# Moving four queues of a three-stage hybrid block onto tables of places, and B's rows into another buffer

## The chip, the cores and the metric

One core of a Trainium2 chip runs the whole program in one launch. The metric is the device time of one execution in microseconds, the median over timed runs. PE is TensorE, PEld its weight loads, DVE VectorE, ACT ScalarE, POOL GpSimd, SP SyncE.

## The reference

Sixteen sequences of 512 tokens of 256 numbers pass through attention, a routed feed-forward layer, a state-space layer, and the feed-forward layer again, each on the layer norm of x and added to x. All inputs are float32.

```
x = x + attention(layernorm(x))     # 16 heads of 16, causal softmax, RMS norm in front
x = x + ffn(layernorm(x))           # base + shared + 2 of 6 routed low-rank experts
x = x + ssm(layernorm(x))           # below
x = x + ffn(layernorm(x))
# ssm: xc = silu(conv4(x)); dt = softplus(xc Wd); B = xc Wb; C = xc Wc     (16 states)
#   h[n,t] = exp(a[n] dt[t]) h[n,t-1] + dt[t] xc[t] B[n,t];   y[t] = sum_n h[n,t] C[n,t]
#   out = (y * sigmoid(x Wg)) Wo
```

## The kernel before

**Frames and places.** The kernel is a software pipeline over the 16 sequences. Its clock is a count of places: 20 places are a group of four heads (10 score units of 2 places), 80 places (`FRAME`) one sequence. Each engine has its queue, written out in the order of places; a table per engine (`PE_AT`, `ACT_AT`, `DVE_AT`, `POOL_AT`, `SP_AT`) says at which place of a sequence a step is issued, and `due(now, at)` which sequence that concerns. Only the order comes from places; when something runs follows from the queues and the semaphores. While one sequence is in attention, the one before is in its state-space layer, and the heads' scores, the maxima and the exponentials (`max_unit`, `score_unit`, `exp_unit`) run between everything else.

**Attention.** Q and K are cast into three bfloat16 parts (`cast_part`, L826), which SP stores in DRAM (`store_parts`, L712) and loads as a stack (`stack`, L726). PE makes scores for the maxima (L372) and for the exponentials (L395); DVE reduces the first (L1026, L1028, L1023), and `finish_maxima` turns the maxima into rows `hlt` (L1044) that SP puts under the stack (`stack_maxima`, L733, four small transfers). ACT takes the exponentials (`pt`, L795), PE multiplies with V (L420).

**The state-space layer.** ACT copies B's 16 rows from a bank into `hwt` (`bc_high`, L878), SP stores them in DRAM (`store_b`, L737) and loads each row, spread over 128 partitions, into one of three buffers `b_all` (`load_b`, L747). ACT makes softplus (L903), DVE from it dt and u (`delta_u`, L1129 and L1131). For each of 16 states n: ACT makes the decays (`dec`, L910, two halves, buffers n % 2), POOL the inputs (`inp` = u times B, L1331 and L1337), DVE the scan (L1158), PE spreads C's row (L557), DVE multiplies (L1167), and POOL adds the product to y by an accumulating transfer (`add_state`, L1344). POOL's queue is in order: inputs 0 and 1 of a sequence stand before the last addition (n = 15) of the sequence before. Then `gate_y` (L1173) multiplies y with the gate and waits for that addition, PE applies the output weights (`ssm_out`, L321 and L323), and DVE adds to X (`add_and_sum`, L1081).

`hwt` is also the buffer for the weighted low-rank tokens of the feed-forward layer (`copy_weighted`, L862), so that copy waits for B's store.

The scans, decays, inputs, loads of B and the group's pieces are not in the tables: every engine's loop runs over groups q and units p, and small maps (`STEP_AT`, `PRODUCT_AT`, `DECAY_AT`, `FINISH`, `HEADS_PE`) say at which unit they stand. In SP's loop the store and first loads of B stand in the side work of unit 7, and the maxima behind it:

```
for now in (2 * (UN * q + p), 2 * (UN * q + p) + 1):
    ...
    if (a := due(now, SP_AT["store_b"])) >= 0:
        store_b(a)
        for n in range(3):
            load_b(NS * a + n)
if p == 7 and 0 <= q + 1 < NQ:
    stack_maxima(q + 1)
```

Of the kernel before, what the change touches and what calls it, by code (L numbers as in the profile page):

```python
# [7 lines left out]
ALU = mybir.AluOpType  # L8
# [48 lines left out]
def hybrid_block(nc, x, norm_w, wqk_t, bqk_c, wv_t, bv, wo_t, bo, conv_w, conv_b, wd_t, bd, wbc_t,  # L57
# [24 lines left out]
    LK = 32  # L82
# [6 lines left out]
    STEP_AT = {0: 0, 2: 1, 5: 2, 7: 3}  # L89
    PRODUCT_AT = {1: 0, 3: 1, 6: 2, 8: 3}  # L90
    DECAY_AT = {1: -1, 4: 0, 5: 1, 8: 2}
# [4 lines left out]
    FRAME = 2 * UN * NG  # L96
    PE_AT = {"res": (-32, -31), "xn": (-75, -71), "qk00": (-52, -50, -48), "qk01": (-50, -47, -44), "v": (-26, -32),
# [7 lines left out]
    ACT_AT = {"res": (-30, -28), "square_f": 98, "square_s": 127, "square_l": 252, "norm_q": -94, "norm_f": 103,  # L105
              "exp0": 115, "norm_s": 131, "softplus": 153, "decays": 160, "norm_l": 257, "exp1": 266,
# [4 lines left out]
    DVE_AT = {"add_x1": (94, 96), "in0": 113, "out0": 116, "add_up0": (123, 124), "silu": 144, "delta": 155,  # L111
              "gated": 246, "add_x3": (251, 251), "in1": 265, "out1": 268, "add_up1": (277, 280), "stats_q": -102}
    POOL_AT = {"rsqrt_f": 99, "rsqrt_s": 124, "rsqrt_q": -104, "inputs": 151, "rsqrt_l": 254, "low": (111, 266)}
    SP_AT = {"parts": (-43, -4), "load_x": -119, "store_b": 155, "store": 281}
    FINISH = 14
    HEADS_PE, HEADS_DVE = 4, 4

    ctx = ExitStack()
    with ctx:
# [88 lines left out]
        b_rows = hwt[0:NS, :]  # L208
# [94 lines left out]
        def _(pe):  # L303
# [246 lines left out]
            def spread_c(k):  # L550

                s, n = divmod(k, NS)
                if has(s):
                    pe.wait_ge(hc_done.sem, hc_done.at(s, n))
                    if n == 0:
                        pe.wait_ge(side["bc"].free, side["bc"].at("bc", s, 2))
                    mm(spread_bank[:, :], onehot[:, NS + n:NS + n + 1].to_broadcast([3 * NC, P]), bcs[:, s % 2, :],  # L557
                       start=True, stop=True).then_inc(c_ready.sem, 1)

            def spread_b(k):  # L560

                s, n = divmod(k, NS)
# [8 lines left out]
            def sum_y(k):  # L571

                s, n = divmod(k, NS)
                if has(s) and s >= LATE:
# [4 lines left out]
                    for c, m in enumerate(late_banks(s)):  # L579
                        last = mm(m[:, :], ident[:, :], hc[:, k % HC, c, :], start=(n == 0), stop=(n == NS - 1),  # L580
                                  skip_group_check=True)
# [72 lines left out]
            for q in range(FIRST, END):  # L654
                k = NG * q - LK
                if q == -2:
                    pe.wait_ge(dve_const, 1)
                for p in range(UN):
                    if 0 <= UN * q + p + LM < UN * NQ:
                        max_unit(UN * q + p + LM)  # L660
                    side_work(2 * (UN * q + p))
                    if 0 <= q < NQ:
                        score_unit(q, p)
                    if p in PRODUCT_AT:
                        spread_b(k + PRODUCT_AT[p] + 1)
                        spread_c(k + PRODUCT_AT[p])
                        sum_y(k + PRODUCT_AT[p] - 1)
                    if 0 <= q - 1 < NQ:
                        if p == 0:
                            values_b(q - 1)  # L670
                        elif p == 1:
                            values_c(q - 1)
                        if p == HEADS_PE:
                            turn_heads(q - 1)
                    if p == 7 and 0 <= q < NQ:
                        values_a(q)
                    side_work(2 * (UN * q + p) + 1)
# [3 lines left out]
        def _(sp):  # L681
# [57 lines left out]
            def load_b(k):  # L739

                s, n = divmod(k, NS)
                if has(s):
                    old_s, old_n = divmod(k - 3, NS)
                    sp.wait_ge(inp_ready.sem, inp_ready.at(old_s, old_n + 1))
                    if n < 3:
                        sp.wait_ge(b_stored.sem, b_stored.at(s))
                    sp.dma_start(b_all[:, k % 3, :], b_kept[s, n][None, :].to_broadcast([P, T])  # L747
                                 ).then_inc(b_loaded[k % 3].sem, 16)
# [11 lines left out]
            for q in range(FIRST, END):  # L760
                k = NG * q - LK
                for p in range(UN):
                    if p < 3 and 0 <= q + 2 < NQ:
                        stack(q + 2, p)
                    if p in STEP_AT and (k + STEP_AT[p]) % NS < NS - 3:
                        load_b(k + STEP_AT[p] + 3)
                    for now in (2 * (UN * q + p), 2 * (UN * q + p) + 1):
                        for j in range(2):
                            if (a := due(now, SP_AT["parts"][j])) >= 0:
                                store_parts(a, j)  # L770
                        if (a := due(now, SP_AT["store"])) >= 0:
                            store(a)
                        if (a := due(now, SP_AT["load_x"])) > 0:
                            load_x(a)
                        if (a := due(now, SP_AT["store_b"])) >= 0:
                            store_b(a)
                            for n in range(3):
                                load_b(NS * a + n)
                    if p == 7 and 0 <= q + 1 < NQ:
                        stack_maxima(q + 1)  # L780
# [4 lines left out]
        def _(act):  # L785
# [126 lines left out]

            def decays_ahead(k):
                s, n = divmod(k, NS)
                if has(s) and n + 2 < NS:
                    decays(s, n + 2)


            def side_work(now):
# [74 lines left out]
            for q in range(FIRST, END):  # L994
                k = NG * q - LK
                if q == -1:
# [5 lines left out]
                for p in range(UN):  # L1002
                    side_work(2 * (UN * q + p))
                    if 0 <= q < NQ:
                        exp_unit(q, p)
                    if p == 2 and 0 <= q - 1 < NQ:
                        copy_heads(q - 1)
                    if p in DECAY_AT:
                        decays_ahead(k + DECAY_AT[p])
                    side_work(2 * (UN * q + p) + 1)  # L1010
# [3 lines left out]
        def _(dve):  # L1014
# [125 lines left out]
            def scan(k):  # L1140
                s, n = divmod(k, NS)
                if k == NS * (NB - 1):
                    half_of_inputs(0)
                if has(s):
                    old_s, old_n = divmod(k - HC, NS)
# [122 lines left out]
            for q in range(FIRST, END):  # L1268
                if q == -4:
                    constants()  # L1270
# [164 lines left out]
```

## Time and profile before

| | |
|---|---|
| timed runs, median (lowest to highest) | 2170.35 us (2165.85 to 2177.23), 3 runs |
| profiled execution, first to last instruction | 2159.4 us, granted clock 0.956 |
| busy | PE 1842.8 us (85%), DVE 1684.1 (78%), ACT 1407.4 (65%), POOL 1040.1 (48%) |
| transfers | 275.53 MB, 128 GB/s; SP's queue 30.5%, POOL's 27.6% of 16 engines |

The profiled execution's own time is its span of 2159.4 us with the start and end of the program around it, which the profile doesn't show. The rows are of that one execution; times in them count from its first instruction. A number in brackets behind an instruction is how long its engine idled before it, and the name behind it is what ended that.

### The profile page before, as it was taken

The numbers are of one execution on the slowest core, as the hardware profiler recorded it, in microseconds if no ns is written. First come the engines' busy times: TensorE is split into PE (matmuls) and PEld (weight loads), VectorE is DVE, ScalarE is ACT, GpSimd is POOL, SyncE is SP. The second block draws the span as 40 slices with busy tenths as digits, with TensorE's granted clock in tenths as the row PEclk, the third lists the DMA queues.
The fourth block names the chain that finished last, engine by engine and source line by source line (L and its number), as shares of the span: only waits on it lengthen the run. The fifth ranks groups of instructions, "written<-read, shape, count | busy, mean of one in ns | idle before, by whom it ended". The sixth has DMA issues, their size and how long they took to land.

```text
span 2159.4 us, 33647 instructions
## 1 busy us (share of the span) xinstructions
PE 1842.8 (85%) x11409; PEld 1132.2 (52%) x11440; DVE 1684.1 (78%) x2586; ACT 1407.4 (65%) x2724; POOL 1040.1 (48%) x930
## 2 busy tenths in 40 slices
PE   5779888998989798988989898898989898877775
PEld 3446454645556464645556464655656464635333
DVE  5343678889788888879787888879887888987783
ACT  2445767686676767677675867677675767574531
POOL 0000364556555464646555464646555464666430
PEclk8999999999999999999999999999999999999998
DMA  4312377666767576667767686666767676652110
GB/s 115 83 52 59 93 152 153 145 142 150 159 140 159 124 170 140 151 128 154 158 148 157 129 171 130 146 142 149 156 141 157 133 157 135 139 112 61 45 59 10
DMA packets 185916, 275.53 MB, mean 128 GB/s; under 512 B 33537, under 2 KB 125586, under 8 KB 185746
## 3 DMA queue, kind: packets, MB, share of 16 engines
q1 hardware_dynamic: 155506, 163.27, 30.5%
q0 software_dynamic: 30240, 110.11, 27.6%
q8 instruction: 92, 1.51, 0.3%
q14 instruction: 78, 0.64, 0.1%
HBM read 128.58 MB, written 34.08 MB: 75 GB/s over the span
## 4 chain that ended last, share of the span: by engine, by line
PE 44%; ACT 19%; DMA 16%; SPq 7%; issue 6%; DVE 5%; POOL 2%; ACTq 0%; POOLq 0%; DVEq 0%
PE bank L314 7%; DMA sk<-qk_parts 7%; PE bank L518 5%; PE bank L323 5%; SPq L726 5%; ACT dec L910 3%; PE bank L372 3%; ACT pt L795 3%; PE bank L395 3%; PE bank L420 3%; PE bank L501 3%; DMA qk_parts<-parts 3%; DMA out<-X 3%; PE bank L482 3%; PE bank L308 2%
## 5 line engine op out<-in xcount | busy, mean ns | idle before, releaser
L1158 DVE TENSOR_TENSOR_SCAN hc<-dec,inp 128x1024 f32<-128x1024 f32 x256 | 613.1, 2395 | 33.0 <-ACT dec L910 28.6
L1331 POOL TENSOR_TENSOR inp<-u,b_all 128x512 f32<-128x512 f32 x256 | 341.1, 1332 | 421.9 <-DVE hc L1158 177.5
L795 ACT ACTIVATE pt<-bank 128x512 f32<-128x512 f32 x640 | 373.8, 597 | 220.4 <-PE bank L397 217.6
L372 PE MATMUL bank<-sk,sq 96*128 96x512 bf16 (+3 forms) x1024 | 279.6, 312 | 95.4 <-DMA sk<-qk_parts 64.4
L1337 POOL TENSOR_TENSOR inp<-u,b_all 128x512 f32<-128x512 f32 x240 | 350.0, 1458 | 18.8
L910 ACT ACTIVATE dec<-dt,a_neg 128x511 f32<-128x511 f32 x512 | 338.0, 717 | 31.4 <-DVE hc L1158 31.4
L1167 DVE TENSOR_TENSOR hc<-hc,bank 128x1024 f32<-128x1024 f32 x242 | 293.6, 1213 | 50.6 <-PE bank L557 49.9
L395 PE MATMUL bank<-sq,sk 98*128 98x512 bf16 (+3 forms) x1024 | 275.4, 307 | 34.1 <-ACT pt L795 28.1
L1344 POOL DMA_DIRECT2D y<-hc x210 | 185.6, 884 | 244.8 <-DMA y<-hc 122.9
L1026 DVE TENSOR_REDUCE mall<-bank 128x1 f32<-128x512 f32 x256 | 172.6, 674 | 100.3 <-PE bank L374 100.0
L372 PEld LDWEIGHTS bank<-sk,sq 96*128 96x128 bf16 x1024 | 102.3, 100 | 213.9 <-DMA sk<-qk_parts 73.0
L1028 DVE TENSOR_REDUCE mall<-bank 128x4 f32<-128x512 f32 x256 | 175.1, 684 | 44.8 <-PE bank L374 44.6
L374 PE MATMUL bank<-mask_qk,ident_bf 128*128 128x128 bf16 x1024 | 199.0, 226 | 0.0
L397 PE MATMUL bank<-mask_kq,ident_bf 128*128 128x128 bf16 x1024 | 196.7, 224 | 0.0
L420 PE MATMUL bank<-pt,v_sb 128*32 128x512 f32 (+3 forms) x2048 | 180.5, 448 | 0.0
L314 PE MATMUL bank<-xt_q,wqk 128*128 128x512 f32 x256 | 127.7, 623 | 42.4 <-ACT parts L826 22.9
L826 ACT ACTIVATE parts<-bank,bqk 128x512 bf16<-128x512 f32 x192 | 128.5, 689 | 53.2 <-PE bank L314 50.0
L395 PEld LDWEIGHTS bank<-sq,sk 98*128 98x128 bf16 x1024 | 102.6, 100 | 113.3 <-ACT pt L795 39.8
L1309 POOL TENSOR_TENSOR rs<-va,half 128x4 f32<-128x4 f32 x64 | 66.3, 1036 | 160.9 <-DVE ng L1068 156.9
L1081 DVE SCALAR_TENSOR_TENSOR X<-bank,X 128x256 f32<-128x256 f32 x192 | 73.2, 418 | 87.1 <-PE bank L502 45.3
L397 PEld LDWEIGHTS bank<-mask_kq,ident_bf 128*128 128x128 bf16 x1024 | 103.1, 101 | 49.2 <-issue 35.5
L1023 DVE TENSOR_REDUCE mall<-bank 128x2 f32<-128x512 f32 x128 | 87.9, 687 | 48.5 <-PE bank L374 48.3
(168 smaller groups left out, 3534.2 us busy)
## 6 DMA issues: line engine op xcount, KB each, us to landing
y<-hc POOLq DMA_DIRECT2D x210, 512.0 KB, 5.5
b_all<-b_kept SPq DMA_DIRECT2D x256, 256.0 KB, 4.0
qk_parts<-parts SPq DMA_DIRECT2D x96, 256.0 KB, 2.5
sq<-qk_parts SPq DMA_DIRECT2D x384, 64.0 KB, 3.6
sk<-qk_parts SPq DMA_DIRECT2D x384, 64.0 KB, 3.8
X<-in_x SPq DMA_DIRECT2D x16, 512.0 KB, 5.9
out<-X SPq DMA_DIRECT2D x16, 512.0 KB, 5.9
sq<-hlt SPq DMA_DIRECT2D x256, 2.0 KB
```

Source lines behind the costliest of these rows:

```text
L314: last = mm(dst[:, :], w[:, c, g * P:(g + 1) * P], src[:, c, :], start=(c == 0), stop=(c == C - 1))
L372: mm(dst[:, o:o + n], sq[0:KS, slot, h, qb * P:(qb + 1) * P], sk[0:KS, slot, h, 0:n], start=True, stop=False)
L374: return mm(dst[:, o + n - P:o + n], ident_bf[:, :], mask_qk[:, :], start=False, stop=True)
L395: mm(dst[:, o:o + n], sk[:, slot, h, kb * P:(kb + 1) * P], sq[:, slot, h, kb * P:T], start=True, stop=False)
L397: return mm(dst[:, o:o + P], ident_bf[:, :], mask_kq[:, :], start=False, stop=True)
L420: last = mm(pv_bank[VW * i:VW * (i + 1), kb * P:T], values_of(a, kb, first + i), pt[:, n % PT, at:at + T - kb * P], start=start, stop=stop ...
L795: A(pt[:, n % PT, :], score_bank[unit % 2][:, :], ACT.Exp).then_inc(exp_done.sem, 1)
L910: last = A(dec[:, n % 2, c, 1:T], dt[:, c, 1:T], ACT.Exp, scale=a_neg[:, c, n:n + 1])
L1158: V.tensor_tensor_scan(h, d, v, 0.0, ALU.mult, ALU.add).then_inc(scan_done.sem, 1)
L1167: V.tensor_tensor(hc[:, k % HC, :, :] if n or s >= LATE else y[:, s % 2, :, :], hc[:, k % HC, :, :], spread_bank[:, None, :].to_broadcast( ...
L1331: first = G.tensor_tensor(inp[:, n % 2, 0, :], u[:, 0, :], b_all[:, k % 3, :], ALU.mult)
L1337: G.tensor_tensor(inp[:, n % 2, 1, :], u[:, 1, :], b_all[:, k % 3, :], ALU.mult).then_inc(inp_ready.sem, 1)
```

## The change

The maps and the loops over q and p go; each engine runs over places `now`, and scans, products, decays, inputs, additions, loads of B, stacks, maxima, values and heads have rows in the tables, with `steps()` and `group()` beside `due()`. B's rows are copied into the first 16 partitions of `tok_f`, the normalised tokens' buffer, and no longer into `hwt`; the wait for B's store moves from `copy_weighted` to `squares`, which next writes `tok_f`. Two waits are new (`stats_q`, `project_v`).

```diff
+    SP_AT = {"parts": (-43, -4), "load_x": -119, "store_b": 155, "store": 281, "stack": (-40, -38, -36),
+             "maxima": -6, "load_b": (155, 155, 155, 160, 164, 170, 174, 180, 184, 190, 194, 200, 204, 210, 214, 220)}
...
-        b_rows = hwt[0:NS, :]
+        b_rows = tok_f[0:NS, 0:2, :].rearrange("p t d -> p (t d)")
...
+        def group(now, at):
+
+            g, rest = divmod(now - at, HALF)
+            return g if rest == 0 and 0 <= g < NQ else -1
+
+        def steps(now, at):
+
+            return [(a, n) for n in range(NS) if (a := due(now, at[n])) >= 0]
...
             def project_v(a, j):
                 m = side["v", j]
+                if a == 0:
+                    pe.wait_ge(dve_const, 1)
...
+            for now in range(START, STOP):
+                for third in range(3):
+                    if (g := group(now, SP_AT["stack"][third])) >= 0:
+                        stack(g, third)
+                if (a := due(now, SP_AT["store_b"])) >= 0:
+                    store_b(a)
+                for a, n in steps(now, SP_AT["load_b"]):
+                    load_b(a, n)
...
+                if (g := group(now, SP_AT["maxima"])) >= 0:
+                    stack_maxima(g)
...
             def squares(b, kind, name, junk):
 
+                if kind == KIND_F:
+                    act.wait_ge(b_stored.sem, b_stored.at(b - 1))
...
                 act.wait_ge(m.full, m.at("hw", b, f))
-                stored = min(b + 1, NB - 1) if f else b - 1
-                if stored >= 0:
-                    act.wait_ge(b_stored.sem, b_stored.at(stored))
...
-                if (a := due(now, ACT_AT["decays"])) >= 0:
-                    decays(a, 0)
-                    decays(a, 1)
...
+                side_work(now)
+                unit, odd = divmod(now, 2)
+                if not odd and 0 <= unit < UN * NQ:
+                    exp_unit(*divmod(unit, UN))
+                if (g := group(now, ACT_AT["heads"])) >= 0:
+                    copy_heads(g)
+                for a, n in steps(now, ACT_AT["decays"]):
+                    decays(a, n)
...
                 if (a := due(now, DVE_AT["stats_q"])) > 0:
+                    dve.wait_ge(xhat[KIND_Q].sem, xhat[KIND_Q].at(a - 1))
```

The order of instructions on PE, DVE and POOL is the same in both kernels. It differs on SP and ACT, each at one place of a frame, in the 14 frames in which the next sequences' attention still runs.

SP's queue from the last transfers of a stack through place 155 to the next stack, before:

```order
L726 DMA sk<-qk_parts 16x4x512
L737 DMA b_kept<-hwt 16x512
L747 DMA b_all<-b_kept 128x512 x3
L733 DMA sq<-hlt 2x16x32 x4
L712 DMA qk_parts<-parts 128x2x512 x3
```

and in the changed kernel:

```order
L737 DMA sk<-qk_parts 16x4x512
L744 DMA sq<-hlt 2x16x32 x4
L748 DMA b_kept<-tok_f 16x512
L757 DMA b_all<-b_kept 128x512 x3
L723 DMA qk_parts<-parts 128x2x512 x3
```

The four transfers of the maxima stood behind B's store and first three loads and now stand ahead of them.

ACT's queue around place 160, where `pt` is the softmax exponential and `dec` the decays of states 0 and 1, before:

```order
L795 ACTIVATE pt<-bank1 128x512
L826 ACTIVATE parts<-bank6,bqk 128x512
L826 ACTIVATE parts<-bank7,bqk 128x512
L910 ACTIVATE dec<-dt,a_neg 128x511 x4
L795 ACTIVATE pt<-bank0 128x512
L795 ACTIVATE pt<-bank1 128x512
```

and in the changed kernel:

```order
L801 ACTIVATE pt<-bank1 128x512
L834 ACTIVATE parts<-bank6,bqk 128x512
L834 ACTIVATE parts<-bank7,bqk 128x512
L801 ACTIVATE pt<-bank0 128x512
L915 ACTIVATE dec<-dt,a_neg 128x511 x4
L801 ACTIVATE pt<-bank1 128x512
```

One exponential stood behind the four instructions of the decays and now stands ahead of them.

## Rows read from the trace of the kernel before

**Rows 1.** The page: span, POOL's transfer queue, chain by engine, issues of y's additions.

```profile
span 2159.4 us, 33647 instructions
...
q0 software_dynamic: 30240, 110.11, 27.6%
...
PE 44%; ACT 19%; DMA 16%; SPq 7%; issue 6%; DVE 5%; POOL 2%; ACTq 0%; POOLq 0%; DVEq 0%
...
y<-hc POOLq DMA_DIRECT2D x210, 512.0 KB, 5.5
```

**Rows 2.** Line L1131 (u): count, ns min/median/max, first and last start.

```profile
L1131 DVE TENSOR_TENSOR u<-dt,xc x16: 1224/1225/1226, 236.1 to 2039.7; 128x1024 f32<-128x1024 f32 x16
```

**Rows 3.** Chain of waits in four frames: start us, us, what.

```profile
498.54 0.79 DVE X L1081 x4
...
981.85 3.72 DMA sk<-qk_parts
...
988.06 0.79 DVE X L1081 x4
...
1843.03 0.79 DVE X L1081 x4
```

**Rows 4.** Timeline of DVE, three frames: start us, us, instruction [idle before].

```profile
972.95 2.29 DVE L1158 TENSOR_TENSOR_SCAN hc<-dec,inp 128x1024 f32<-128x1024 f32 x1 [1.88 <-ACT dec L910]
...
980.64 1.21 DVE L1173 SCALAR_TENSOR_TENSOR y<-gate,y 128x1024 f32<-128x1024 f32 x1
...
1355.46 0.42 DVE L1081 SCALAR_TENSOR_TENSOR X<-bank,X 128x256 f32<-128x256 f32 x1 [2.40 <-PE bank L323]
...
1598.27 0.42 DVE L1081 SCALAR_TENSOR_TENSOR X<-bank,X 128x256 f32<-128x256 f32 x1 [1.93 <-PE bank L323]
```

**Rows 5.** Timeline of SP, 954 to 965 us.

```profile
954.92 0.32 SPq L737 DMA_DIRECT2D b_kept<-hwt  x1
957.72 1.35 SPq L747 DMA_DIRECT2D b_all<-b_kept  x3
961.89 3.21 SPq L733 DMA_DIRECT2D sq<-hlt  x4
```

**Rows 6.** Waits: who waited for whom, us in total, times, longest.

```profile
POOL inp L1331 <- DVE u L1131: 100.7, 14, 23.0
...
ACT hwt L862 <- PE bank L490: 86.3, 32, 6.3
...
SPq L733 <- DVE hlt L1044: 421.9, 64, 15.1
```

**Rows 7.** B's first load (issued 957.7), then the addition to y (issued 972.6).

```profile
DMA to landing us min/median/max: 3.3/3.3/3.3
...
DMA to landing us min/median/max: 6.2/6.2/6.2
```

**Rows 8.** Timeline of POOL, 967 to 973 us.

```profile
967.21 1.26 POOL L1331 TENSOR_TENSOR inp<-u,b_all 128x512 f32<-128x512 f32 x1 [5.61 <-DVE u L1131]
968.55 1.28 POOL L1337 TENSOR_TENSOR inp<-u,b_all 128x512 f32<-128x512 f32 x1
...
972.56 0.86 POOL L1344 DMA_DIRECT2D y<-hc  x1
```

**Rows 9.** Timeline of PE, 974 to 986 us.

```profile
974.67 0.39 PE L395 MATMUL bank<-sq,sk 98*128 98x512 bf16 x1 [1.01 <-ACT pt L795]
...
985.62 0.39 PE L372 MATMUL bank<-sk,sq 96*128 96x512 bf16 x1 [1.58 <-DMA sk<-qk_parts]
```

**Rows 10.** Timeline of ACT, 974 to 975 us.

```profile
974.02 1.09 ACT L795 ACTIVATE pt<-bank 128x512 f32<-128x512 f32 x2
```

**Rows 11.** Windows: length, busy us by engine, then clock, DMA share, GB/s.

```profile
967.90:971.80 3.90, 3.80 (x40) 2.10 (x39) 2.42 (x3) 3.90 (x8) 3.57 (x4) 1.00 0.00 0
...
978.70:982.70 4.00, 3.76 (x25) 2.99 (x23) 4.00 (x4) 3.21 (x6) 0.11 (x1) 0.72 0.95 177
...
1353.00:1356.40 3.40, 3.38 (x12) 2.25 (x11) 1.00 (x7) 0.09 (x1) 2.07 (x2) 0.50 0.65 129
```

More of the change, by code:

```diff
@@ L548, in ssm_delta, with spread_c, spread_b @@
                 by_columns(m.tile, wd, xc, g).then_inc(m.full, 1)
[L550 to L562, printed above, removed]
+            def spread_c(s, n):
+                pe.wait_ge(hc_done.sem, hc_done.at(s, n))
+                if n == 0:
+                    pe.wait_ge(side["bc"].free, side["bc"].at("bc", s, 2))
+                mm(spread_bank[:, :], onehot[:, NS + n:NS + n + 1].to_broadcast([3 * NC, P]), bcs[:, s % 2, :],
+                   start=True, stop=True).then_inc(c_ready.sem, 1)
+            def spread_b(s, n):
                 if s == NB - 1:
@@ L569, in spread_b, with sum_y @@
                        start=True, stop=True).then_inc(b_ready.sem, 1)
-            def sum_y(k):
-                s, n = divmod(k, NS)
-                if has(s) and s >= LATE:
+            def sum_y(s, n):
+                if s >= LATE:
                     if n == 0:
@@ L579, in sum_y @@
                     for c, m in enumerate(late_banks(s)):
-                        last = mm(m[:, :], ident[:, :], hc[:, k % HC, c, :], start=(n == 0), stop=(n == NS - 1),
+                        last = mm(m[:, :], ident[:, :], hc[:, (NS * s + n) % HC, c, :], start=(n == 0), stop=(n == NS - 1),
                                   skip_group_check=True)
@@ L653, in _ @@
             pe.wait_ge(folded, 1)
-            for q in range(FIRST, END):
-                k = NG * q - LK
-                if q == -2:
+            for now in range(START, STOP):
+                if now == -2 * HALF:
                     pe.wait_ge(dve_const, 1)
[L658 to L677, printed above, removed]
+                unit, odd = divmod(now, 2)
+                if not odd and 0 <= unit + LM < UN * NQ:
+                    max_unit(unit + LM)
+                side_work(now)
+                if not odd and 0 <= unit < UN * NQ:
+                    score_unit(*divmod(unit, UN))
+                for a, n in steps(now, PE_AT["b"]):
+                    spread_b(a, n)
+                for a, n in steps(now, PE_AT["c"]):
+                    spread_c(a, n)
+                for a, n in steps(now, PE_AT["sum"]):
+                    sum_y(a, n)
+                if (g := group(now, PE_AT["values"][1])) >= 0:
+                    values_b(g)
+                if (g := group(now, PE_AT["values"][2])) >= 0:
+                    values_c(g)
+                if (g := group(now, PE_AT["heads"])) >= 0:
+                    turn_heads(g)
+                if (g := group(now, PE_AT["values"][0])) >= 0:
+                    values_a(g)
         @block.sync
@@ L759, in _ @@
                 sp.dma_start(dst, src).then_inc(w_rest, 16)
[L760 to L780, printed above, removed]
+            for now in range(START, STOP):
+                for third in range(3):
[5 more added lines that the diff above has]
+                    load_b(a, n)
+                for j in range(2):
+                    if (a := due(now, SP_AT["parts"][j])) >= 0:
+                        store_parts(a, j)
+                if (a := due(now, SP_AT["store"])) >= 0:
+                    store(a)
+                if (a := due(now, SP_AT["load_x"])) > 0:
+                    load_x(a)
+                if (g := group(now, SP_AT["maxima"])) >= 0:
+                    stack_maxima(g)
             sp.wait_ge(x_stored.sem, x_stored.at(NB - 1))
@@ L993, in _ @@
             A(ex[:, 0, 0:1], ident[:, 0:1], ACT.Exp)
-            for q in range(FIRST, END):
-                k = NG * q - LK
-                if q == -1:
+            for now in range(START, STOP):
+                if now == -HALF:
                     act.wait_ge(dve_const, 1)
@@ L1001, in _ @@
                     act.wait_ge(act_own.sem, act_own.one())
[L1002 to L1010, printed above, removed]
+                side_work(now)
+                unit, odd = divmod(now, 2)
+                if not odd and 0 <= unit < UN * NQ:
+                    exp_unit(*divmod(unit, UN))
[3 more added lines that the diff above has]
+                    decays(a, n)
         @block.vector
@@ L1138, in half_of_inputs, with scan @@
                 V.tensor_tensor(inp[:, n % 2, 1, :], pv_bank[:, :], u[:, 1, :], ALU.mult).then_inc(b_used.sem, 1)
[L1140 to L1142 removed]
+            def scan(s, n):
+                k = NS * s + n
+                old_s, old_n = divmod(k - HC, NS)
+                if s == NB - 1 and n == 0:
                     half_of_inputs(0)
[L1144 to L1158 removed]
@@ new lines, in scan @@
+                dve.wait_ge(dec_ready.sem, dec_ready.at(s, n + 1))
+                dve.wait_ge(inp_ready.sem, inp_ready.at(s, n + 1))
+                if s == NB - 1:
+                    dve.wait_ge(b_used.sem, b_used.at(0, n + 1))
+                if old_s >= LATE:
+                    dve.wait_ge(y_summed.sem, y_summed.at(old_s - LATE, old_n + 1))
+                elif old_n == 0:
+                    dve.wait_ge(hc_done.sem, hc_done.at(old_s, 1))
+                else:
+                    dve.wait_ge(y_added.sem, y_added.at(old_s, old_n))
@@ L1267, in _ @@
             dve.sem_inc(folded, 1)
-            for q in range(FIRST, END):
-                if q == -4:
+            for now in range(START, STOP):
+                if now == -4 * HALF:
                     constants()
-                k = NG * q - LK
-                for p in range(UN):
-                    if 0 <= UN * q + p + LM < UN * NQ:
-                        maximum(UN * q + p + LM)
-                    if FINISH == 2 * p and 0 <= q + 1 < NQ:
-                        finish_maxima(q + 1)
-                    if p == HEADS_DVE and 0 <= q - 1 < NQ:
-                        head_norm(q - 1)
-                    side_work(2 * (UN * q + p))
-                    if p in STEP_AT:
-                        scan(k + STEP_AT[p])
-                    if p in PRODUCT_AT:
-                        product(k + PRODUCT_AT[p])
-                    if FINISH == 2 * p + 1 and 0 <= q + 1 < NQ:
-                        finish_maxima(q + 1)
-                    side_work(2 * (UN * q + p) + 1)
+                unit, odd = divmod(now, 2)
+                if not odd and 0 <= unit + LM < UN * NQ:
+                    maximum(unit + LM)
+                if (g := group(now, DVE_AT["finish"])) >= 0:
+                    finish_maxima(g)
+                if (g := group(now, DVE_AT["heads"])) >= 0:
+                    head_norm(g)
+                side_work(now)
+                for a, n in steps(now, DVE_AT["scan"]):
+                    scan(a, n)
+                for a, n in steps(now, DVE_AT["product"]):
+                    product(a, n)
         @block.gpsimd
@@ L1345, in add_state @@
                                accum_op=ALU.add).then_inc(y_added.sem, 16)
-            def after_step(k):
-                s, n = divmod(k, NS)
-                if has(s) and n + 2 < NS:
-                    inputs(s, n + 2)
-                if has(s) and n and s < LATE:
-                    add_state(s, n)
             G.memset(ident[:, :], 0.0)
@@ L1386, in side_work @@
                         weigh_low(a, f)
-                if (a := due(now, POOL_AT["inputs"])) >= 0:
-                    inputs(a, 0)
-                    inputs(a, 1)
-            for q in range(FIRST, END):
-                if q == -4:
-                    pool.wait_ge(dve_const, 1)
-                for p in range(UN):
-                    side_work(2 * (UN * q + p))
-                    if p in STEP_AT:
-                        after_step(NG * q - LK + STEP_AT[p])
-                    side_work(2 * (UN * q + p) + 1)
+            for now in range(START, STOP):
+                if now == -4 * HALF:
+                    pool.wait_ge(dve_const, 1)
+                side_work(now)
+                for a, n in steps(now, POOL_AT["inputs"]):
+                    inputs(a, n)
+                for a, n in steps(now, POOL_AT["add"]):
+                    if n and a < LATE:
+                        add_state(a, n)
 def kernel(**inputs):
```

79 lines of the change are left out of this document (32 added, 47 removed), and 19 rows, old and new, of tables (ACT_AT, PE_AT).

## The prediction

> **What bounds the kernel now.** I read the page first [rows 1]. TensorE (PE) is busy most, but the chain that ended last spends only 44% of the span on it; 19% is on ScalarE (ACT), 16% on transfers, 7% on SyncE's queue (SP). No engine is the bound by itself: the order of the queues and the waits between them set the period of a frame (80 places, one sequence, 1803.6 us over 15 of them or 120.2 us [rows 2]), so a delay counts only where the chain passes. I therefore went to the one stretch of a frame where the order changes, places 154 to 171, and read it in the frame that has it at 954 to 989 us.
>
> There the chain of waits [rows 3] leaves ACT with the last cast of Q and K, goes through the store of the parts and SP's loads of the stack, whose last lands at 985.57 (981.85 + 3.72), then through PE to the VectorE (DVE) addition L1081 at 988.06. That addition is where two paths meet. One is the transfer path just named. The other is DVE alone: from the scan at 972.95 its timeline has no idle mark through the gating product to that addition [rows 4], so whatever delays that scan, or the gating product at 980.64, arrives at 988.06 in full. The addition stands on the chain in seven of the 14 frames concerned, first at 498.54, last at 1843.03 [rows 3]. In the other seven it stays with PE and transfers there, and DVE has time in hand, as the 2.40 us that it idles before the addition at 1355.46 [rows 4].
>
> **SP: the maxima go ahead of B.** Before, SP stores B's rows at 954.92, issues three loads of them from 957.72, and then waits for the maxima, which it issues at 961.89 for 3.21 us [rows 5]. That it waits there for DVE's transposed maxima and for nothing else is what the waits say, 64 times for 64 groups [rows 6]. So the maxima win nothing by going first: they leave at 961.89 either way. B's rows lose. They can be stored only at 961.89 + 3.21 = 965.10; from the store's issue to the first load's was 957.72 - 954.92 = 2.80 us, so the first load leaves at 967.90, and such a load took 3.3 us to land [rows 7]: 971.2. GpSimd (POOL) now starts input 0 at 967.21, because it waits for u, not for B [rows 8]; the waits say so 14 times [rows 6]. After the change it starts at 971.2: **4.0 us later**. It is the same in each of the 14 frames, since the maxima and u are tied to one another on DVE by one scan and the two steps of delta.
>
> The Trainium skill, page "DMA: Bandwidth & Descriptors", section "Anatomy of one DMA", puts a transfer at about 2.0 us plus its bytes at 436 GB/s. By that the 32 KB store takes 2.1 us and a 256 KB load 2.6, the shift is 2.6 us in place of 4.0, the gating product would be 0.7 late, and the whole change would come to some +9 us. The trace has 2.80 and 3.3 for these very transfers, so the measured ones stand.
>
> What hangs on POOL's 4.0 us:
> - The first scan. Input 0 is two halves, done at 969.8 (968.55 + 1.28) before [rows 8] and 973.8 after; the scan started at 972.95 behind ACT's decays [rows 4]. It moves by 1.0.
> - The last addition of the sequence before to y, a transfer that stands behind inputs 0 and 1 in POOL's queue: 972.56 before [rows 8], 976.6 after. It took 6.2 us to land [rows 7], so 978.8 before and 982.8 after. DVE's gating product waits for it and started at 980.64 [rows 4] with 1.9 us in hand. It starts at 982.8: **2.1 us late**. This takes the scan's 1.0 in; they do not add.
> - PE's first half of the output projection waits for the gating product. PE then idles 1.58 us at 985.62 for the stack [rows 9], which hides all but 0.5.
> - Input 2 and the loads of B for steps 3 to 5 are late by less than they had in hand: the latter stand behind the stack's loads in SP's queue, as before.
>
> **ACT: one softmax exponential goes ahead of four decays.** Two exponentials behind the decays took 1.09 us [rows 10], so the decays of state 0 come 0.5 us later and with them, at the least, the scan. That lies under the 1.0 from POOL. If B were not moved, it would be the cost, 0.5 us a frame. In return PE gets its exponential sooner and loses the 1.01 us of idling at 974.67 [rows 9]; but its next maxima wait for DVE's reduction behind the late scan, so I give this nothing. That is the gain excluded here and priced below.
>
> **Transfers.** The addition to y occupies 27.6% of 2159.4 us over its 210 issues [rows 1], which is 2.84 us of all 16 engines each. Moved by 4.0 of its 6.2 us, it takes about 1.8 us of work out of a stretch before 976.6 and puts it beside the stack's loads, where the DMA share is 0.95 already [rows 11]. The three loads of B do the reverse: they move from a busy stretch into one where the share is 0.00 [rows 11], and cost nothing. So the stack's last landing, which carries the chain in the seven other frames, is late by 0 at best and by 1.8 - 0.2 = 1.6 at worst. I take 0.9, a little over the middle because the share is nearly full.
>
> **Costed at nothing.** The rows of B in the normalised tokens' buffer are the same copy and transfer. The wait that is taken from the copy of the weighted tokens ended nothing: 86.3 us of its idling, 32 times of 32, went to PE's transposes [rows 6]. The new waits are for things long done: the squares (place 98) wait for the B store of the sequence before (155 - 80 = 75), 23 places or some 35 us earlier; the statistics (-102) for tokens normalised at -174; the values for constants that PE has waited for 8 places before anyhow. The tables place everything else where it was.
>
> **The sum.** Seven frames at 2.1, less 1.9 for the one of them in which DVE idles 1.93 before the addition, at 1598.27 [rows 4]: 12.8 us. Seven at 0.9: 6.3. Together +19 us, and 2159.4 becomes 2178.5 for the profiled span. The timed runs lie 6 to 18 us above that span, at a median of 2170.35, so I forecast **2190 us**, 0.9% slower. I take 0.5% (2159.5 to 2181.2) as what a measurement of this kernel can tell from no change.
>
> **The rivals.**
> - *Forecast*, chance 0.60: 2183 by a stack that is not late at all, 2194 by one 1.6 late, and some 3 us on either side for a frame's own slack in the addition to y.
> - *Contention*, 0.12: the moved addition is itself slowed by the stack's loads by 1.6, and gating comes 3.7 late. 7 x 3.7 - 1.9 + 7 x 1.6 = +35, 2205. For it speaks the share of 0.95; against it, that the first of the loads are issued one by one by SP and not by capacity. The same page of the Trainium skill, section "Issuing engines are not separate DMA queues", says that transfers from SP and GpSimd run on the same 16 engines and interleave, which speaks for this one; no row here shows these two together at full overlap.
> - *Absorbed*, 0.20: the period is set by the transfer path in nearly every frame and the stack lands as before; DVE's lateness is taken up by idling like the 2.40 us at 1355.46. Then +0 to +6, 2170 to 2176. Against it stands the addition L1081 on the chain seven times.
> - *Faster*, 0.08: one mechanism, PE's 1.01 us at 974.67. If B's rows came less than 1.9 us late (the hand of the gating product), DVE would not be pushed by POOL, the stretch would be paced by PE's scores, and 14 x 1.0 gives 2156. It decides if the store and first load together take under 4.0 us and not 6.1.
>
> The range reaches from the absorbed case to past the contended one, 2168 to 2210. What lies within it is about 0.8. Slower by over 0.5%: 0.69 (the forecast nearly whole, contention). Within: 0.23 (absorbed, the forecast's edge). Faster: 0.08.
>
> **What would show it.** In the profile after: SP's order maxima, store, loads, with the store some 3.2 us after the maxima start. POOL's input 0 waiting for B's load in 14 frames and no more for u, 4.0 us after u (5.6 us of POOL idle become about 9.6). The first scan waiting for POOL's inputs, not for the decays, and the idle time before it up from 1.88 to 2.9. The gating product L1173, which waits nowhere in these frames now, waiting for the addition to y by about 1 us beyond that, 13 times. A frame of 121.5 us. I am wrong if the maxima are issued before 961.9 relative to u (then they did bind SP), if gating does not wait, or if L1081 keeps its time against the stack's landing although gating waited: then the seven frames' slack was larger than the chain says. The clock is a loose end: behind each such idle stretch of PE some frames show it at 0.50 (1353.0 to 1356.4 [rows 11]), the lower of its two levels, and more idling before the output projection could bring it there in more of them.

## The result and the profile after

The changed kernel takes **2204.07 us** (median of four runs, 2199.31 to 2207.5) against 2168.10 us before (four runs): a ratio of 1.017, 95% interval 1.0135 to 1.0205. It is slower, as forecast, and inside the range, but by some 36 us where the sum said 19. Of all the runs told of here one lay in the slower state (2186.25 us, in experiment 1); the ratios leave it out. The profiled span went from 2159.4 to 2200.2 us, a frame (from u to u, over 15 of them) from 120.2 to 122.8, the mean granted clock of PE from 0.956 to 0.941.

Lines have new numbers: L744 issues the maxima, L748 stores B's rows, L757 loads them, L723 stores the parts, L737 loads the stack; L1320 and L1326 are POOL's input halves, L1333 the addition to y; L1151 is the scan, L1159 the product with C, L1165 the gating product, L1075 the addition to X, L1125 is u; L915 is the decays, L801 the exponentials; L335 and L337 are PE's output projection.

The page of the changed kernel, rows that answer to [rows 1] (and the costliest groups with their idle time):

```profile
span 2200.2 us, 33633 instructions
...
PE 44%; DMA 17%; ACT 14%; DVE 8%; SPq 7%; issue 5%; POOL 5%; POOLq 0%; DVEq 0%; ACTq 0%
...
L1320 POOL TENSOR_TENSOR inp<-u,b_all 128x512 f32<-128x512 f32 x256 | 350.5, 1369 | 406.5 <-DMA b_all<-b_kept 156.6
...
L1326 POOL TENSOR_TENSOR inp<-u,b_all 128x512 f32<-128x512 f32 x240 | 394.4, 1643 | 18.8
```

ACT lost five points of the chain, DVE and POOL won three each. The second half of a product, L1326, now takes 1643 ns in the mean. The same group before had a mean of 1458 already, though the halves in [rows 8] took 1.26 and 1.28 us:

```profile
L1337 POOL TENSOR_TENSOR inp<-u,b_all 128x512 f32<-128x512 f32 x240 | 350.0, 1458 | 18.8
```

The waits of the changed kernel (us in total, times, longest), to be read beside [rows 6]:

```profile
POOL inp L1320 <- DMA b_all<-b_kept: 156.6, 22, 25.2
...
POOL inp L1320 <- DVE u L1125: 11.6, 2, 10.7
...
DVE y L1165 <- DMA y<-hc: 31.5, 14, 4.1
...
DVE hc L1151 <- ACT dec L915: 36.8, 18, 2.7
```

Input 0 waited 14 times for u, 100.7 us in all; now u is left with two waits, and B's loads have the rest. The gating product waits 14 times for the addition to y, 31.5 us. One of these waits, 3.9 us at 1985, lies behind the 14 frames and was there before (4.0 us at 1948); the first of the 14 frames has no sequence before it to gate. The new waits are the other 13, 27.6 us, 2.1 each. The first scan still waits for the decays, not for POOL.

One frame of the changed kernel, SP, then POOL, then DVE (start us, us, instruction, [idle before]); it answers to [rows 4, 5, 8]:

```profile
977.89 3.21 SPq L744 DMA_DIRECT2D sq<-hlt  x4
981.14 0.41 SPq L748 DMA_DIRECT2D b_kept<-tok_f  x1
982.84 1.74 SPq L757 DMA_DIRECT2D b_all<-b_kept  x3
987.78 1.43 SPq L723 DMA_DIRECT2D qk_parts<-parts  x3
...
986.68 1.27 POOL L1320 TENSOR_TENSOR inp<-u,b_all 128x512 f32<-128x512 f32 x1 [9.07 <-DMA b_all<-b_kept]
988.03 1.28 POOL L1326 TENSOR_TENSOR inp<-u,b_all 128x512 f32<-128x512 f32 x1
989.48 3.32 POOL L1320 TENSOR_TENSOR inp<-u,b_all 128x512 f32<-128x512 f32 x1 [0.17 <-POOL inp L1326]
992.88 1.27 POOL L1326 TENSOR_TENSOR inp<-u,b_all 128x512 f32<-128x512 f32 x1
994.09 0.87 POOL L1333 DMA_DIRECT2D y<-hc  x1
...
981.91 1.23 DVE L1125 TENSOR_TENSOR u<-dt,xc 128x1024 f32<-128x1024 f32 x1
...
989.45 2.29 DVE L1151 TENSOR_TENSOR_SCAN hc<-dec,inp 128x1024 f32<-128x1024 f32 x1 [2.37 <-ACT dec L915]
...
1001.23 1.56 DVE L1165 SCALAR_TENSOR_TENSOR y<-gate,y 128x1024 f32<-128x1024 f32 x1 [4.12 <-DMA y<-hc]
```

SP does what the prediction said: maxima, store 3.25 us later, loads. u is done at 983.14 and input 0 starts 3.5 us after it. The third row of POOL is the one the prediction does not have: a half of input 1 that starts 0.03 us into the first scan takes 3.32 us instead of 1.27. In 11 of the 13 frames it is the other half of input 1 that is caught so, for 3.13 us. The addition to y so leaves 10.95 us after u is done; before it was about 5.4 (972.56 less 967.1, [rows 8]).

The chain of waits through the same frame (start us, us, what):

```profile
981.14 1.64 DMA b_kept<-tok_f
...
982.84 3.71 DMA b_all<-b_kept
...
989.48 3.32 POOL inp L1320
...
992.88 1.21 POOL inp L1326
994.09 7.12 DMA y<-hc
...
1001.23 1.57 DVE y L1165
...
1002.84 0.40 PE bank L335
1003.24 1.71 PE bank L337 x4
...
1008.97 0.88 PE bank L337 x4
...
1009.88 0.79 DVE X L1075 x4
```

From SP's maxima to the addition to X nothing but the delayed path is left; Q and K's parts and the stack, which carried this frame in [rows 3], are off it. In 11 of the 14 frames the chain runs this way; three (the first, which has nothing to gate, the third and the twelfth) stay with the stack. Of the output projection the four matmuls at 1003.24 take 1.71 us, the last four 0.88.

The windows of the same frame (length, busy us by engine, then clock, DMA share, GB/s) show why, beside [rows 11]:

```profile
996.00:1001.20 5.20, 2.09 (x13) 1.26 (x11) 1.11 (x2) 3.35 (x6) 4.87 (x4) 0.81 1.10 202
1002.80:1006.90 4.10, 4.06 (x11) 2.88 (x12) 4.07 (x6) 0.00 (x0) 0.88 (x1) 0.50 0.61 161
```

PE is busy for 2.09 of 5.20 us ahead of the gating product, and the projection behind it runs at a granted clock of 0.50, the 1.2 GHz level. Its first four matmuls behind a gating product are at that level 13 times of 14, and were 2 times before (the last of the 14, at 1985 and 1948, in both kernels).

### The profile page after: what moved, and what is told of

Its sections match the earlier page's. It is cut to its first block, busy times and chain, and to the rows that moved or that the text cites. A ratio compares the mean times of both kernels' runs of the same rounds, so it can differ in the third digit from the quotient of the medians.

```text
span 2200.2 us, 33633 instructions
## 1 busy us (share of the span) xinstructions
PE 1859.1 (84%) x11409; PEld 1143.9 (52%) x11440; DVE 1695.2 (77%) x2586; ACT 1407.5 (64%) x2724; POOL 1088.8 (49%) x930
## 4 chain that ended last, share of the span: by engine, by line
PE 44%; DMA 17%; ACT 14%; DVE 8%; SPq 7%; issue 5%; POOL 5%; POOLq 0%; DVEq 0%; ACTq 0%
PE bank L328 7%; PE bank L337 6%; PE bank L534 5%; DMA sk<-qk_parts 5%; DMA y<-hc 4%; SPq L737 3%; DMA out<-X 3%; PE bank L388 3%; PE bank L436 3%; SPq L744 3%; PE bank L411 3%; PE bank L498 3%; PE bank L517 3%; ACT dec L915 3%; PE bank L322 2%
## 5 line engine op out<-in xcount | busy, mean ns | idle before, releaser
L1151 DVE TENSOR_TENSOR_SCAN hc<-dec,inp 128x1024 f32<-128x1024 f32 x256 | 618.3, 2415 | 41.3 <-ACT dec L915 36.8
L1320 POOL TENSOR_TENSOR inp<-u,b_all 128x512 f32<-128x512 f32 x256 | 350.5, 1369 | 406.5 <-DMA b_all<-b_kept 156.6
L801 ACT ACTIVATE pt<-bank 128x512 f32<-128x512 f32 x640 | 376.0, 598 | 247.9 <-PE bank L413 244.9
L1326 POOL TENSOR_TENSOR inp<-u,b_all 128x512 f32<-128x512 f32 x240 | 394.4, 1643 | 18.8
L915 ACT ACTIVATE dec<-dt,a_neg 128x511 f32<-128x511 f32 x512 | 338.2, 719 | 29.7 <-DVE hc L1151 29.7
L1159 DVE TENSOR_TENSOR hc<-hc,bank 128x1024 f32<-128x1024 f32 x242 | 293.7, 1213 | 49.9 <-PE bank L571 49.4
L1333 POOL DMA_DIRECT2D y<-hc x210 | 185.9, 885 | 250.5 <-DVE hc L1159 137.5
L1075 DVE SCALAR_TENSOR_TENSOR X<-bank,X 128x256 f32<-128x256 f32 x192 | 73.3, 419 | 77.9 <-PE bank L518 42.9
```

What stands on the lines that cost most here:

```text
L801: A(pt[:, n % PT, :], score_bank[unit % 2][:, :], ACT.Exp).then_inc(exp_done.sem, 1)
L915: last = A(dec[:, n % 2, c, 1:T], dt[:, c, 1:T], ACT.Exp, scale=a_neg[:, c, n:n + 1])
L1151: V.tensor_tensor_scan(h, d, v, 0.0, ALU.mult, ALU.add).then_inc(scan_done.sem, 1)
L1159: V.tensor_tensor(hc[:, k % HC, :, :] if n or s >= LATE else y[:, s % 2, :, :], hc[:, k % HC, :, :], spread_bank[:, None, :].to_broadcast( ...
L1320: first = G.tensor_tensor(inp[:, n % 2, 0, :], u[:, 0, :], b_all[:, k % 3, :], ALU.mult)
L1326: G.tensor_tensor(inp[:, n % 2, 1, :], u[:, 1, :], b_all[:, k % 3, :], ALU.mult).then_inc(inp_ready.sem, 1)
```

## The experiments

The kernel before ran again beside each group: 2165.45 us (25 runs) for the first four, 2163.94 (21) for the next three, 2167.52 (8) for the last. Ratios are to it; they differ a little from the quotients of the medians.

**1. SP's order put back**, everything else as changed.

```
-    SP_AT = {... "maxima": -6, ...
+    SP_AT = {... "maxima": -5, ...
```

> The changed kernel with SP's queue as before (B's store and first three loads ahead of the maxima); the exponential stays ahead of the first decays, and B's rows stay in tok_f. Theory (the late B rows are the whole cost, by way of POOL's queue and the addition to y): about 2168 to 2175 us, since only the decays' 0.5 us in 14 frames is left, +7 at most. Rival (the exponential ahead of the decays carries a share): 2180 or more. Rival (ACT's swap is a gain hidden by SP's loss, PE's 1.01 us of idling): 2155 to 2162.

2155.67 us, ratio 0.9957 (0.9929 to 0.9985). The whole loss is gone, and a little more: the expected 2168 to 2175 were missed, and the time is where the rival had it by which ACT's swap is a gain. The waits of PE in this kernel, of which [rows 9] shows one from before:

```profile
PE bank L411 <- ACT pt L801: 13.3, 20, 5.1
...
PE bank L388 <- DVE mall L1020: 36.4, 24, 2.5
```

Before, by the same view, PE idled 28.1 us (34 times) for the exponentials and 15.1 us (23 times) for that maximum. The early exponential does remove PE's idling of 1.01 us, and PE then idles for DVE's maxima instead, as the prediction had it, which gave the earlier exponential nothing.

**2 and 3. ACT's order put back**, alone and together with SP's:

```
                 side_work(now)
+                for a, n in steps(now, ACT_AT["decays"]):
+                    if n < 2:
+                        decays(a, n)
                 unit, odd = divmod(now, 2)
                 if not odd and 0 <= unit < UN * NQ:
                     exp_unit(*divmod(unit, UN))
...
                 for a, n in steps(now, ACT_AT["decays"]):
-                    decays(a, n)
+                    if n >= 2:
+                        decays(a, n)
```

> The changed kernel with ACT's queue as before (the decays of states 0 and 1 ahead of the exponential); SP keeps the maxima ahead of B's store. Theory (B late is the cost): 2200 to 2206 us, as the changed kernel's 2204, because POOL's inputs and the addition to y come just as late. Rival (ACT's swap carries a share): 2190 or less.

> The changed kernel with both queues as before: what is left of the change is B's rows in tok_f, the moved wait and the two new waits. Theory (these cost nothing): 2168 us, within 0.3% of before. Rival (a new wait or the buffer binds somewhere): over 2180.

Alone: 2205.67 us, ratio 1.0216 (1.0172 to 1.026), no better than the changed kernel. With SP's order too: 2163.97 us, 0.9988 (0.9954 to 1.0022), no difference from before. So SP's swap is the whole loss, and B's rows in the other buffer, with the waits that moved, cost nothing that can be measured. The exponential's place is worth nothing in the changed kernel, and with SP's order back some 8 us that are not clear of noise (2155.67 against 2163.97, intervals that overlap).

**4. The last addition to y ahead of inputs 0 and 1** in POOL's queue, SP as changed.

```
-               "inputs": (151, 151, 160, ...
+               "inputs": (155, 155, 160, ...
```

> The changed kernel with POOL's inputs 0 and 1 placed behind the last addition to y of the sequence before (places 155, 155 in place of 151, 151). SP and ACT stay changed, so B's rows are as late. Theory (the loss goes through the addition to y and the gating product): the addition leaves right behind the last product, about 7 us sooner, the gating product waits no more, and the time falls to 2175 to 2188 us. Rival (the loss goes through the late first scan): 2200 or more, as input 0 is no earlier.

2180.05 us, 1.0092 (1.0058 to 1.0125): 24 us less than the changed kernel, two thirds of the loss by the medians and about half by the ratios, and the gating product waits for nothing. The wait for the addition is thus a cause. POOL's timeline of this kernel, and then its three stores of the parts in another frame (from issue to landing):

```profile
974.77 0.85 POOL L1333 DMA_DIRECT2D y<-hc  x1 [8.55 <-DVE hc L1159]
...
978.45 3.27 POOL L1320 TENSOR_TENSOR inp<-u,b_all 128x512 f32<-128x512 f32 x1 [0.17 <-POOL inp L1326]
```

```profile
DMA to landing us min/median/max: 3.4/3.7/4.0
```

The half of input 1 is long here too, and the stores of the parts, ahead of which the addition now leaves, take 3.7 us; in the changed kernel they take 2.5 to 3.1. That this makes the part of the loss that remains is argued from 7 and 8, not shown here. A second part is in the trace: the gating product itself takes 1.65 us in each of the 13 frames, where it took 1.21 before; it starts while the long half still runs.

**5. The first scan waits for inputs 0 and 1**, not for 0 alone, SP as changed. This puts nothing else elsewhere; it only keeps the scan off POOL's halves.

```
-                dve.wait_ge(inp_ready.sem, inp_ready.at(s, n + 1))
+                dve.wait_ge(inp_ready.sem, inp_ready.at(s, 2 if n == 0 and s < LATE else n + 1))
```

> The changed kernel, in which the first scan of each sequence (up to the 14th) waits for inputs 0 and 1, not for 0 alone. In the changed kernel's trace the second half of input 1 starts inside that scan and takes 3.08 us where it takes 1.27 elsewhere, and the addition to y stands behind it. Theory (that stretch of 1.8 us is what the prediction missed, and the gating product carries it): the half takes 1.3 us, the addition leaves 1.8 sooner, the gating product starts 1.4 to 1.9 sooner though the first scan starts 2.7 later, and the time falls by 12 frames of about 1.4 us to 2185 to 2192 us. Rival (the stretch is harmless or not due to the scan): 2204 or more.

2185.77 us, 1.0092 (1.0071 to 1.0114), though a wait was added to the kernel. Its POOL and DVE, then the start of its output projection:

```profile
975.97 1.27 POOL L1320 TENSOR_TENSOR inp<-u,b_all 128x512 f32<-128x512 f32 x1 [9.05 <-DMA b_all<-b_kept]
...
978.77 1.27 POOL L1320 TENSOR_TENSOR inp<-u,b_all 128x512 f32<-128x512 f32 x1 [0.17 <-POOL inp L1326]
980.12 1.26 POOL L1326 TENSOR_TENSOR inp<-u,b_all 128x512 f32<-128x512 f32 x1
981.32 0.87 POOL L1333 DMA_DIRECT2D y<-hc  x1
...
981.47 2.29 DVE L1151 TENSOR_TENSOR_SCAN hc<-dec,inp 128x1024 f32<-128x1024 f32 x1 [5.08 <-issue]
...
991.36 0.28 PE L335 MATMUL bank<-rows_w,pick 96*128 96x256 bf16 x1 [0.84 <-DVE y L1165]
```

The half takes 1.27 us again and the addition leaves 2 us sooner after input 0 (5.35 against 7.41). A scan that starts some 2.7 us later (it idles 5.08 us and not 2.37) costs less than what it removes: 18 us less than the changed kernel, half of the loss. But the 18 us are not the price of the long half alone. The gating product waits for nothing now, and yet starts only 0.5 us sooner after u in the mean of 13 frames (16.6 us against 17.1), where 1.4 to 1.9 were expected, because the scan in front of it is held. The rest is gained behind it, where the output projection now runs at the full clock in most frames (see the loose end below).

**6. B's store ahead of the maxima**, its three loads behind them.

```
-    SP_AT = {... "store_b": 155, ...
+    SP_AT = {... "store_b": 154, ...
```

> The changed kernel with B's store ahead of the maxima and only its three loads behind them. B's first load then leaves at the end of the maxima, 2.8 us sooner than in the changed kernel, and input 0 is about 1.2 us late against before where it was about 3.4. Theory (the addition to y has 1.9 us in hand, a late B within that is free): as with SP's queue fully back, 2153 to 2165 us, the gating product waiting nowhere. Rival (each us of lateness costs in proportion, 14 x 1.2): 2170 or more.

2154.93 us, 0.9978 (0.9946 to 1.0011). SP and POOL:

```profile
1074.18 3.49 SPq L744 DMA_DIRECT2D sq<-hlt  x4
1077.79 1.31 SPq L757 DMA_DIRECT2D b_all<-b_kept  x3
...
1081.13 1.27 POOL L1320 TENSOR_TENSOR inp<-u,b_all 128x512 f32<-128x512 f32 x1 [7.23 <-DMA b_all<-b_kept]
...
1083.92 1.27 POOL L1320 TENSOR_TENSOR inp<-u,b_all 128x512 f32<-128x512 f32 x1 [0.17 <-POOL inp L1326]
```

Input 0 still waits for B, but is only about 1.6 us later than u allows (7.23 us of idling against 5.61 in [rows 8]; 1.2 to 2.0 over the 13 frames), and gating does not wait in them. The point from which lateness costs lies between: up to 2.0 us is free, 2.9 to 3.5 us is not.

**7. SP's order back, and the addition to y between inputs 0 and 1** (`"inputs": (151, 155, 160, ...`): an attempt to gain from the other side.

> SP's queue as before, ACT's exponential ahead (as in the first experiment, 2156 us), and POOL's input 1 behind the last addition to y of the sequence before, so that this addition leaves about 2.7 us sooner and is down before the stack's last loads. Theory (the addition beside the stack's loads delays the stack, which carries the chain in half of the frames): 2140 to 2152 us. Rival (the stack's landing goes by SP's issues, not by the engines' load): 2156, no change, or a little slower by a late input 1.

2174.91 us, 1.0046 (1.0022 to 1.0069): a miss. It is 19 us slower than experiment 1, although the addition leaves sooner and gating has time in hand. The stores of the parts in one frame, first of experiment 1, then of this one (the median of the three over the 13 frames is 2.5 to 3.1 us there and 3.7 to 4.6 here):

```profile
DMA to landing us min/median/max: 2.2/2.5/2.8
```

```profile
DMA to landing us min/median/max: 3.5/3.7/4.1
```

**8. The same, with the addition cut to half its bytes.** The second half of y lacks the product of state 15.

```
+                cs = slice(0, 1) if n == NS - 1 else slice(0, C)
-                pool.dma_start(y[:, s % 2, :, :], hc[:, (NS * s + n) % HC, :, :],
+                pool.dma_start(y[:, s % 2, cs, :], hc[:, (NS * s + n) % HC, cs, :],
```

> The kernel of the run before (maxima back behind B's loads, input 1 behind the last addition to y), with that last addition cut to the first of its two halves: 256 KB in place of 512 KB; the second half of y lacks the product of state 15. In the run before, the addition left 1.6 us ahead of the stores of the parts (1099.83 and 1101.4), the three stores landed 3.8, 4.1 and 3.5 us after their issue where they took 2.2, 2.7 and 2.4 with the addition behind the first of them, and the kernel took +19 us. Theory, contention: the stores and the stack behind them lie in the queues of the 16 DMA engines behind the addition's bytes. Half the bytes are half of its 2.84 us of all engines, so the stores should land in about 2.4 to 2.9 us and the kernel be 9 to 15 us faster than the run before: 2158 to 2166 (2152 to 2160 if all of the loss is the last 1.4 us). Rival, order: the loss comes from input 1, which is now done about 1 us later behind the addition (the second scan, GpSimd's queue, or the addition's issue ahead of the others), and the bytes do not matter: the stores still take 3.5 us or more, or they are quick again and the time stays at 2170 to 2180.

2153.91 us, 0.9932 (0.9895 to 0.9969), 21 us less than experiment 7 (25 by the ratios). The addition and the first two stores are issued as they were there (the first store 1.6 us behind; the third comes 2.6 us behind and not 3.4), input 1 is still behind the addition, and the stores of one frame land so (2.9 to 3.4 us over the frames, 4.3 in the first):

```profile
DMA to landing us min/median/max: 2.5/2.9/3.0
```

So it is the bytes of the addition ahead of the stores, not the order of POOL's work. The gain is larger than the 9 to 15 us expected, and why is not shown: half the bytes took away the whole of the 19 us by which 7 was slower than 1. The Trainium skill, page "DMA: Bandwidth & Descriptors", section "Issuing engines are not separate DMA queues", has the transfers of SP and GpSimd interleave on the same 16 engines, and these rows agree.

## Why the prediction was right, and where its size was off

**SP and B's rows: right.** Maxima, then the store 3.25 us later, then the loads. The shift of input 0 was forecast at 4.0 us and is 2.9 to 3.5 (3.5 in the frame shown): the store and the first load's issue took 982.84 - 981.14 = 1.70 us and not the 2.80 of [rows 5]. The load itself took 3.71, more than 3.3. The Trainium skill's estimate (page "DMA: Bandwidth & Descriptors", section "Anatomy of one DMA") is one for transfers that GpSimd issues, and these leave from SP. It gives 2.1 us for the store, which landed in 1.64, and 2.6 for the load, which took 3.71; neither sum would have given the time.

**What hangs on POOL: the path right, the price too small.** This is the step that was mis-sized: "976.6 after", the departure of the addition to y as input 0's lateness and nothing more. In the frame shown it is 5.5 us late (10.95 - 5.4): 3.5 from B, and 2.0 from the half of input 1 that now lies in the first scan. The landing took 7.1 us in place of 6.2. Against 1.9 us in hand that makes 5.5 + 0.9 - 1.9 = 4.5 us of delay, and the row has 4.12 of idling behind a scan that is 0.5 later. In the mean of the 13 frames the sum is 3.0 us from B, 1.9 from the long half and 0.5 of landing, less 1.8 in hand: gating starts 3.6 us later, where the prediction had 2.1. Its idling is 0.7 to 4.1 us, 27.6 in all, where I had about 1 us each. Besides, the gating product itself takes 1.61 us in the mean and not 1.21, because in six of these frames it starts while one of POOL's halves runs; the prediction has no term for that.

The traces of before could have told it. 29 input halves in it last 2.9 to 3.3 us, and all 29 start inside a scan; in the changed kernel 57 last over 2 us, 54 of which start inside one. I took 1.27 us from halves in a stretch without a scan, and moved them into a stretch with one. That the overlap, and not the lateness as such, makes the half long is shown by experiment 5. Its price is not shown by itself: experiment 5 gave back 18 us, but it also held the scan and brought the clock back.

**The first scan: wrong in cause, harmless.** It waits for the decays as before and comes 0.5 us later, as the exponential makes it; POOL's two halves of input 0 were done at 989.31, 0.14 us before it started. Experiment 1 is no slower than 3, so the exponential's half microsecond costs nothing.

**ACT, the buffer, the moved waits: right.** Experiments 1 to 3.

**The sum.** It let seven frames take the gating delay and seven a stack that is 0.9 us late. The delay is large enough that 11 frames of 14 now run through the addition to y, so the slack of the stack's path was overrun rather than shared. Counted to the end of the addition to X in the mean of the 13 frames, gating starts 3.6 us later and takes 0.4 longer, and what follows it is 0.95 shorter, because the stack is no longer waited for: 3.0 us a frame, 39.5 over 13, beside 40.8 in the span. Of the 3.6 us, 1.9 are the long half. The total agrees with the 2205 of the contention rival, by a different mechanism: what was slowed was POOL's product, not the stack. That rival's premise is real, as 7 and 8 show, but it decides where the addition leaves ahead of the stores of the parts; in the changed kernel it leaves 5.5 to 6.3 us behind the first of them, and they take 2.5 to 3.1 us. The addition itself landed 0.5 us later in the mean of the 13 frames (6.7 against 6.2), not 1.6.

**The loose end.** The lower clock did come: the first four matmuls of the projection at 0.50 behind 13 gating products where they were so behind 2. Over all frames 104 of the projection's matmuls run so, against 49 before. It goes with the idling of PE ahead of the projection, 4.44 us in the frame shown and 0.84 in that of experiment 5: in experiments 4, 5 and 6, where gating does not wait in the frames concerned, it is 2, 2 and 3 times. What it costs can be read against experiment 5. There gating comes 3.1 us later than before too, but the addition to X ends 6.5 us behind it in 10 of the 13 frames, without idling for the projection. In the changed kernel DVE idles for the projection there in 11 of the 13, 6.8 us in all, one of them the twelfth frame, in which PE also waits for the stack:

```profile
1009.88 0.42 DVE L1075 SCALAR_TENSOR_TENSOR X<-bank,X 128x256 f32<-128x256 f32 x1 [1.27 <-PE bank L337]
```

So the lower clock makes an estimated 6 to 7 of the 36 us (from this idling), a term that the prediction named and did not price. No run changed the clock alone.

**The gain on the other side** was priced at 14 us and given 0.08. With the loss undone, experiment 1 is 0.4% faster than before, 2155.67 us where that rival had 2156. PE's idling for the exponentials is halved, but that for the maxima grew by more, so these rows do not explain the gain; against experiment 3 the intervals overlap. What it comes from stays open.

## What to carry to other kernels

Before you move work of GpSimd or VectorE by a few microseconds, look up what the same instruction costs beside each thing that it may come to lie beside: a mean from a quiet stretch is a price for that stretch. A transfer that only one late consumer needs can wait behind others up to that consumer's slack, and no more: here up to 2.0 us was free and 2.9 to 3.5 us cost 1.7% through a queue three steps away. And a large transfer that leaves ahead of a small one on the critical path is paid for by the small one, whichever engine issued it.

## What the runs showed of the hardware

- A GpSimd product of 128x512 from SBUF takes 1.27 us alone. When it starts inside a VectorE scan of 128x1024 it ends 1.06 to 1.08 us after that scan (all 54 long ones in the changed kernel, all 29 before) and so takes 2.9 to 3.3 us. It works both ways: one that starts before the scan keeps its 1.27, and the scan ends 2.14 to 2.16 us after it (where the two overlap by over 0.3 us) and so takes up to 3.5 us instead of 2.29. The Trainium skill, page "SBUF — State Buffer", section "Who interferes with whom", says that a VectorE instruction with two SBUF inputs and a GpSimd instruction that reads SBUF exclude one another, and that the later one blocks until the first is done. The rows agree: in the frame shown the scan ends at 991.74 and the half at 992.80, a little less than one product's time later.
- Three stores of 256 KB, the first issued 1.6 us behind a 512 KB accumulating transfer, land in 3.7 us (median of a frame; 3.7 to 4.6 over the frames of experiment 7), behind one of 256 KB in 2.9 (2.9 to 3.4, 4.3 once; experiment 8), and in 2.5 (2.5 to 3.1; experiment 1) when the accumulating transfer leaves after the first of them.
- The last addition to y, an accumulating transfer of 512 KB, takes 4.6 to 5.7 us from issue to landing when it leaves ahead of the stores (experiments 4 and 7), and 5.6 to 8.0 where the changed kernel issues it.
